# Edge attention in steps of one tile of 128 edges, softmax over 20 tiles at once, and a group's four placements interleaved with queries and relations

## The chip, the cores and the metric

The kernel runs on one core of one Trainium2 chip. The metric is the device time of one execution in microseconds (us). Before the change it is 1203.07 us, the median of three runs (1202.24 to 1210.01).

## The reference

One block of a graph network over 3125 nodes of 256 features, with three parts: attention over edges (4 heads of 64), a linear attention over all nodes, and a mixture of 8 experts of which each node takes two. The change lies in the edge attention. There are 53125 edges, sorted by their target node `dst`; a node's edges stand next to each other.

```
xn = layernorm(x)
Q, K, V = (xn + 0.1*query_emb) @ Wq + bq, ... Wk, ... Wv      # 3125 x 4 x 64
score[e,h] = sum_d Q[dst e] * (K[src e] + 0.2*rel_w[type e]) / 8
w          = softmax of score over the edges that share dst
agg[n]     = sum over edges e with dst e = n of w[e] * V[src e]
x = x + layernorm(agg @ Wo + bo + xn)*gamma + beta + linear_attention(xn)
x = x + experts(layernorm(x))
```

## The kernel before, in words

The program has five stages: projections and the step list (0 to about 170 us), edges (about 170 to 827 us), combination, routing, experts. The stages before and after the edges keep their work, apart from buffer addresses and the sizes of the step list.

**Tiles, steps and groups.** A tile is 128 edges, one per partition. Nodes are handled in 25 blocks of 128. A step holds edges of one block of nodes only, so the step list has one more entry for each change of block: with steps of 256 edges (two tiles) there are 208 + 24 = 232 steps, 464 tiles. The block of a step is known only at run time; its offsets are in one-partition rows in SBUF (`qRow`, `own_bank`, `next_bank`, `aRow`, `last_bank`), and an engine reads them into registers with `load_values` (line 92). A group is four tiles, two steps; there are 116. A chunk of the softmax is four groups, 16 tiles; there are 29.

**Scoring a group.** GpSimd gathers the key and value rows of each tile's sources (516 floats a row) into a ring `KV` of three chunks, 48 tiles, with an indirect DMA for each tile (line 668). Before a gather it waits until the placement of the tile that last had this place is done, and it is at most three groups ahead of the key addition. SyncE loads target and type rows. VectorE makes one-hots of them: `PT` (line 897), and for every second group `OT` (line 901). TensorE multiplies them with the node block's queries (`queries`, line 779, three bf16 parts, two tiles a call) and with the relations (`relations`, line 768). VectorE then adds the relations to the keys (`modify`, line 911), multiplies by the queries (`multiply`, line 918, twice) and sums by head (`reduce`, line 924).

**Softmax of a chunk.** It is a running maximum over edges of one target. TensorE turns the scores (`turn_scores`), VectorE scans them forward and backward (962, 968), the ends of the tiles go over a one-partition row (`turn_ends`, `ends`, `carry`, `carried`, `turn_carries`, `carry_in`), ScalarE takes exponentials (`exponents`), TensorE turns them back (`turn_weights`) and ScalarE copies them to `WS` (`weights`, which waits for its own copies at the end). This is spread over the four groups of the next chunk. When a chunk begins, VectorE rescales the sums so far (`rescale`, line 946).

**Summing.** Two chunks behind the scoring (8 groups), ScalarE multiplies the values by the weights, four activations a tile (`weigh`, line 684); in the last two chunks VectorE does it, two tiles at once (line 937). VectorE makes the placement matrices `PM` (`place`, line 929, two buffers), and TensorE adds the weighted values into one of three PSUM banks by the block of nodes (`aggregate`, line 811). Once a step, TensorE clears the bank that comes next (`clear`, line 798), and ScalarE copies the sums of the bank before to `ACC` (`copy_sums`, line 698); the copy waits for the placement of the step before (`s_pw`) and for its own copy before (`s_acc`).

**Order of the work.** It is written out by hand on each engine and tied by semaphores. In each group TensorE goes: register loads, queries of the first two tiles of the next group, clear and placement of a step, relations of the next group, queries of its last two tiles, clear and placement of the other step. VectorE goes: one-hots of the next group, `modify`, `place`, two `multiply` with small softmax instructions between, `reduce`. ScalarE: for each of two steps `weigh` and `copy_sums`, its register loads (`before`, line 687) once a group. When no group is left to score, the last two chunks are summed (`drain`). Then SyncE's load of the values of nodes (`VB`, line 652), issued when 216 steps are placed, has to be there for the next stage.

## Time and profile before

| | |
|---|---|
| median of the runs | 1203.07 us (1202.24 to 1210.01) |
| the profiled execution's own time | 1205.97 us |
| its span, first to last instruction | 1204.2 us |
| TensorE (PE) busy | 1019.1 us (85%) |
| VectorE (DVE) busy | 909.2 us (76%) |
| ScalarE (ACT) busy | 814.2 us (68%) |
| GpSimd (POOL) busy | 802.1 us (67%) |
| key additions of the edge stage | 116, starting at 184.8 to 795.5 us |

The profiled execution is one run under the hardware profiler; the sums are made against its times. Busy shares are means over stages with different limits. PEld is TensorE's weight load, which overlaps its multiplications; a name that ends in q is an engine's instruction sequencer, which runs ahead of the engine and also reads registers. "idle before <-" names what ended the idle time ahead of an instruction; "issue" is time in which the engine waited for nothing that the profile shows. Instructions of an engine overlap a little: the next starts before the last one is quite done.

### The profile page before, as it was taken

What the parts mean: (1) busy time and instruction counts of PE and PEld (TensorE: products, weight loads), DVE (VectorE), ACT (ScalarE), POOL (GpSimd) and SP (SyncE); (2) the same over time, 40 slices, a digit from 0 to 9 for tenths busy, and PEclk for the clock granted to TensorE, in tenths of its full rate; (3) what the DMA queues carried; (4) which work ended last, traced back from release to release, by engine and by line L of the source; (5) the groups of instructions that cost most, each with busy time, mean ns of one, the idle gap of its engine ahead of it and who ended that gap; (6) DMA issues with size and microseconds to landing.
All of it is one profiled execution on the core that took longest, in us unless ns stands there. A gap on an engine that the chain in (4) does not pass through costs nothing. (4 is left out here: it accounts for less than half of the span.)

```text
span 1204.2 us, 26894 instructions
## 1 busy us (share of the span) xinstructions
PE 1019.1 (85%) x6959; PEld 778.4 (65%) x6960; DVE 909.2 (76%) x1999; ACT 814.2 (68%) x2902; POOL 802.1 (67%) x873
## 2 busy tenths in 40 slices
PE   4899966888888888888888888878996489999993
PEld 3677744565565556555556565556895478999993
DVE  5777547999998999999999999985996823333331
ACT  3344410489888888898988889863675466766662
POOL 3667657777777777777777777712983347666662
PEclk9899975699998999999999999998997689999997
DMA  8333438888888888888888888876325724444445
GB/s 240 114 122 113 141 105 234 240 248 234 240 240 241 243 239 238 243 242 241 246 243 239 247 244 244 242 242 227 111 71 177 237 53 72 69 70 65 70 66 133
DMA packets 130432, 220.56 MB, mean 183 GB/s; under 512 B 24772, under 2 KB 89452, under 8 KB 129992
## 3 DMA queue, kind: packets, MB, share of 16 engines
q0 software_dynamic: 48832, 138.49, 42.9%
q1 hardware_dynamic: 81480, 80.63, 21.5%
q8 instruction: 55, 0.90, 0.3%
q14 instruction: 65, 0.53, 0.1%
HBM read 188.00 MB, written 34.25 MB: 185 GB/s over the span
## 5 line engine op out<-in xcount | busy, mean ns | idle before, releaser
L668 POOL DMA_INDIRECT KV<-kv,ixs x464 | 471.7, 1017 | 151.5 <-issue 110.9
L684 ACT ACTIVATE KV<-KV,WS 128x65 f32<-128x65 f32 x1728 | 437.2, 336 | 40.7 <-issue 40.6
L811 PE MATMUL ps_o<-KV,PM 128*128 128x260 f32 x928 | 255.5, 399 | 49.1 <-DVE PM L929 31.4
L785 PE MATMUL ps_qe<-Q,PT 128*128 x1392 | 209.6, 288 | 21.8 <-DVE PT L897 12.9
L811 PEld LDWEIGHTS ps_o<-KV,PM 128*128 128x128 f32 x928 | 160.4, 193 | 91.5 <-issue 73.0
L785 PEld LDWEIGHTS ps_qe<-Q,PT 128*128 128x128 bf16 x1392 | 122.4, 100 | 77.3 <-issue 46.5
L918 DVE TENSOR_TENSOR KV<-KV,ps_qe 128x512 f32<-128x512 f32 x232 | 149.5, 674 | 0.2
L911 DVE TENSOR_TENSOR KV<-KV,ps_u 128x1024 f32<-128x1024 f32 x116 | 140.0, 1207 | 12.8 <-DMA KV<-kv,ixs 12.5
L924 DVE TENSOR_REDUCE S<-KV 128x16 f32<-128x1024 f32 x116 | 138.7, 1196 | 1.1
L1705 DVE TENSOR_TENSOR YG<-ps_y,KV 128x256 f32<-128x256 f32 x56 | 23.8, 425 | 140.8 <-PE ps_y L1678 140.8
L1589 POOL DMA_INDIRECT acc<-YG,DX x56 | 88.7, 1583 | 61.3 <-issue 36.9
L1619 ACT ACTIVATE HT<-ps_h,WB 128x128 f32<-128x128 f32 x224 | 82.1, 367 | 58.4 <-PE ps_h L1662 45.9
L1662 PE MATMUL ps_h<-XT,WB 128*128 128x128 f32 x896 | 114.9, 282 | 0.0
L1662 PEld LDWEIGHTS ps_h<-XT,WB 128*128 128x128 f32 x896 | 105.8, 194 | 5.2 <-issue 2.4
L1678 PE MATMUL ps_y<-Q,HT 128*128 x448 | 105.8, 379 | 0.0
L698 ACT COPY ACC<-ps_o x231 | 81.6, 353 | 13.5 <-PE ps_o L811 11.2
L1678 PEld LDWEIGHTS ps_y<-Q,HT 128*128 128x128 f32 x448 | 80.9, 190 | 8.7
L775 PEld LDWEIGHTS ps_u<-rel,OT 64*128 64x128 bf16 x1392 | 49.5, 98 | 51.0 <-issue 46.9
L929 DVE TENSOR_TENSOR PM<-iota_f,DC 128x512 f32<-128x512 f32 x116 | 78.5, 677 | 1.7 <-PE ps_o L811 1.7
L1579 POOL DMA_INDIRECT XG<-xtab,GX x56 | 55.5, 992 | 25.5 <-issue 10.1
L775 PE MATMUL ps_u<-rel,OT 64*128 64x64 bf16 x1392 | 63.5, 195 | 10.1 <-DVE KV L911 6.5
L798 PE MATMUL ps_o<-nought 128*128 128x260 bf16 x230 | 63.5, 276 | 0.7 <-ACT ACC L698 0.5
(306 smaller groups left out, 1610.5 us busy)
## 6 DMA issues: line engine op xcount, KB each, us to landing
dlb<-dl_rows SPq DMA_DIRECT2D x116, 128.0 KB
tyb<-ty_rows SPq DMA_DIRECT2D x116, 64.0 KB
KV<-kv,ixs POOLq DMA_INDIRECT x464
kv<-kvb SPq DMA_DIRECT2D x25, 258.0 KB, 2.5
xs_rows<-xs SPq DMA_DIRECT2D x25, 256.0 KB, 2.5
KV<-xs_rows SPq DMA_DIRECT2D x10, 640.0 KB, 9.8
Q<-in_f_W_dram SPq DMA_DIRECT2D x8, 512.0 KB, 6.0
KV<-in_f_W_dram SPq DMA_DIRECT2D x8, 512.0 KB, 6.0
```

Source lines behind the costliest of these rows:

```text
L668: pool.indirect_dma_start(kv[:, c % KR, n, :], None, d["kv"], bass.IndirectOffsetOnAxis(ap=T["ixs"][:, c % KR, n:n + 1], axis=0)).then_inc ...
L684: m = a.activation(part, part, ACT.Copy, scale=W[:, c % 2, s * H + h:s * H + h + 1])
L775: m = pe.matmul(T["ps_u"][:, k * D:(k + 1) * D], T["OT"][half, G_ // 2 % 2, k * P:(k + 1) * P], T["rel3"][half, n, :], start=(n == 0), sto ...
L785: m = pe.matmul(T["ps_qe"][:, p % 3, k, :], T["PT"][:, h, (p % 2 * 2 + k) * P:(p % 2 * 2 + k + 1) * P], T["Q3"][:, bass.ds(at + n * C, C)] ...
L811: m = pe.matmul(ps_o[:, bass.ds(bank, A)], PM[:, p // 2 % 2, p % 2 * 2 + k, :], kv[:, c % KR, 2 * x + k, C:KVW], start=False, stop=True, s ...
L911: v.tensor_tensor(k, k, T["ps_u"][:, 0:G * D].rearrange("p (s d) -> p s d", s=G).unsqueeze(2).broadcast_to([P, G, H, D]), ALU.add).then_in ...
L918: v.tensor_tensor(k, k, T["ps_qe"][:, p % 3, :, :], ALU.mult).then_inc(s_mu, 1)
L924: v.tensor_reduce(S[:, c % 2, g * G * H:(g + 1) * G * H].rearrange("p (s h) -> p s h", h=H), keys(G_).rearrange("p s (h d) -> p s h d", h= ...
L1589: pool.indirect_dma_start(d["acc"], bass.IndirectOffsetOnAxis(ap=T["DX"][:, u, 0:1], axis=0), YG[:, u * C:(u + 1) * C], None, compute_op=A ...
L1619: a.activation(HT[:, u % 2, m, :], T["ps_h"][:, m, 0:SLOTS], ACT.Gelu, bias=WB[:, u % 2, 2 * HID + m:2 * HID + m + 1]).then_inc(s_hg, 1)
L1662: r = pe.matmul(T["ps_h"][:, m, 0:SLOTS], WB[:, u % 2, k * HID + m * P:k * HID + (m + 1) * P], XT[:, u % 2, k, :], start=(k == 0), stop=(k ...
L1678: r = pe.matmul(T["ps_y2"][:, (u % YB) * HB + w, 0:C], HT[:, u % 2, m, w * P:(w + 1) * P], T["W2"][:, bass.ds(at + m * C, C)], start=(m == ...
```

## The change

A step is now one tile of 128 edges. The step list has 416 + 24 = 440 steps and as many tiles, 110 groups of four. A softmax chunk is five groups, 20 tiles; there are 22. The ring keeps 48 tiles, no longer cut into chunks; the gathers take their indices from `SRC` itself, and ScalarE's index copies (line 677) go. Each tile has its own block: `queries` takes an offset for each tile, a bank is cleared and copied once a tile, and TensorE reads `qRow`, `own_bank` and `next_bank` four values at a time, once a group; ScalarE still reads two values at a time, now twice a group. Sums are 9 groups behind the scoring. TensorE's order in a group is: register loads, placement 0, queries, (turned scores), placement 1, relations, placement 2, (turned weights), queries, placement 3, each placement with its clear. VectorE weighs the fourth tile of every odd group, and in the last nine groups tiles 1 to 3. The separate drain is now part of the same loop. Counts in the preparation and the addresses of buffers that share memory with the ring follow; `VB` is loaded once 405 of 440 tiles are placed.

```diff
-TE = 2 * P
+TE = P
 ET = (E_REAL + TE - 1) // TE
 H, D = 4, 64
 NREL = 64
 MD = 32
 NS = ET + NT - 1
-SC = 2
+SC = 4
 SP_ = NS // SC
 G = 4
-CP = 8
-NCH = NS // CP
-CG = 2 * CP // G
-CB_ = 2 * CP
-KR = 3
+CB_ = 20
+NCH = NS // CB_
+CG = CB_ // G
+NG = NS // G
+RING = 48
+LAG = 9
 RO = 3
...
+    CAR, RRO, WO = P + 2 * B, P + 2 * B + 2, P + 2 * B + 8
+    NX = NG + LAG
+    def by_vector(g):
+        if g >= NG - LAG:
+            return ((1, 1), (2, 2))
+        return ((3, 1),) if g % 2 else ()
+    def by_scalar(g):
+        taken = [k + n for k, m in by_vector(g) for n in range(m)]
+        return [k for k in range(G) if k not in taken]
+    scalar_count, vector_count, a_n, v_n = {}, {}, 0, 0
+    for g in range(NG):
+        for k in by_scalar(g):
+            a_n += 1
+            scalar_count[g * G + k] = a_n
+        for k, m in by_vector(g):
+            v_n += 1
+            for n in range(m):
+                vector_count[g * G + k + n] = v_n
...
-            for c in range(NCH):
-                pool.wait_ge(s_ix, c + 1)
-                for g in range(CG):
-                    for k in range(G):
-                        n, scored = g * G + k, c * CG + g - AHEAD
-                        if k % 2 == 0:
-                            wait(pool, s_pw, (c - KR) * CP + 2 * g + k // 2 + 1)
-                        if k == 0:
-                            wait(pool, s_ku, scored + 1)
-                        if k == 2:
-                            wait(pool, s_sc, scored + 1)
-                        pool.indirect_dma_start(kv[:, c % KR, n, :], None, d["kv"],
-                                                bass.IndirectOffsetOnAxis(ap=T["ixs"][:, c % KR, n:n + 1], axis=0)).then_inc(s_g[(c * CG + g) % GS], 16)
+            for t in range(NS):
+                g = t // G
+                wait(pool, s_pw, t - RING + 1)
+                if t % G == 0:
+                    wait(pool, s_ku, g - AHEAD + 1)
+                pool.indirect_dma_start(kv[:, t % RING, :], None, d["kv"],
+                                        bass.IndirectOffsetOnAxis(ap=T["SRC"][:, t:t + 1], axis=0)).then_inc(s_g[g % GS], 16)
         @block.scalar
         def _(a):
-            def indices(c):
-                if c >= KR:
-                    last = (c - KR) * CG + CG - 1
-                    a.wait_ge(s_g[last % GS], 16 * G * (last // GS + 1))
-                a.copy(T["ixs"][:, c % KR, :], T["SRC"][:, c * CB_:(c + 1) * CB_]).then_inc(s_ix, 1)
-            def weigh(p):
-                c, x = divmod(p, CP)
-                for s in (2 * x, 2 * x + 1):
-                    for h in range(H):
-                        part = kv[:, c % KR, s, C + h * (D + 1):C + (h + 1) * (D + 1)]
-                        m = a.activation(part, part, ACT.Copy, scale=W[:, c % 2, s * H + h:s * H + h + 1])
+            def weigh(t):
+                for h in range(H):
+                    part = kv[:, t % RING, C + h * (D + 1):C + (h + 1) * (D + 1)]
+                    at = t % CB_ * H + h
+                    m = a.activation(part, part, ACT.Copy, scale=W[:, t // CB_ % 2, at:at + 1])
                 m.then_inc(s_wv, 1)
...
-                if q % CP == 0:
-                    a.wait_ge(s_rs, q // CP)
+                if q % CB_ == 0:
+                    a.wait_ge(s_rs, q // CB_)
...
+            for x in range(NX):
+                c, j = x // CG - 1, x % CG
+                g = x - LAG
+                softmax, summed = 0 <= c < NCH, g >= 0
+                for k in range(G):
+                    t = g * G + k
+                    if summed:
+                        if k % 2 == 0:
+                            at, bank = before(max(t - 1, 0))
+                        if k in by_scalar(g):
+                            weigh(t)
+                        if t >= 2:
+                            copy_sums(t - 1, at[k % 2], bank[k % 2])
+                    if softmax and j == 1 and k == 1:
+                        ends(c)
+                if softmax and j == 2:
+                    exponents(c)
+                if softmax and j == 3:
+                    weights(c)
+            at, bank = before(NS - 2)
+            copy_sums(NS - 1, at[1], bank[1])
+            a.wait_ge(s_pw, NS)
+            a.wait_ge(s_acc, NS - 1)
...
+                return load_values(nc, mybir.EngineType.PE, T["qRow"][0:1, G * G_:G * G_ + G], (NT - 1) * 3 * C)
+            def banks(name, t, n):
+                return load_values(nc, mybir.EngineType.PE, T[name][0:1, t:t + n], 2 * 512)
...
+            def aggregate(t, bank):
+                g = t // G
+                pe.wait_ge(s_pm, g + 1)
+                if t in vector_count:
+                    pe.wait_ge(s_wd, vector_count[t])
                 else:
-                    pe.wait_ge(s_wv, p + 1)
-                if x == 0:
-                    wait(pe, s_rs, c)
-                for k in range(2):
-                    m = pe.matmul(ps_o[:, bass.ds(bank, A)], PM[:, p // 2 % 2, p % 2 * 2 + k, :], kv[:, c % KR, 2 * x + k, C:KVW],
-                                  start=False, stop=True, skip_group_check=True)
-                m.then_inc(s_pw, 1)
+                    pe.wait_ge(s_wv, scalar_count[t])
+                if t % CB_ == 0:
+                    wait(pe, s_rs, t // CB_)
+                pe.matmul(ps_o[:, bass.ds(bank, A)], PM[:, g % 2, t % G, :], kv[:, t % RING, C:KVW],
+                          start=False, stop=True, skip_group_check=True).then_inc(s_pw, 1)
...
+            for x in range(NX):
+                c, j = x // CG - 1, x % CG
+                g, G_ = x - LAG, x + 1
+                softmax, summed, scored = 0 <= c < NCH, g >= 0, G_ < NG
+                if scored:
+                    at = rows(G_)
+                if summed:
+                    own = banks("own_bank", g * G, G)
+                    after = banks("next_bank", max(g * G - 1, 0), G)
+                    shift = 1 if g == 0 else 0
+                def add(k):
+                    t = g * G + k
+                    if summed:
+                        if t >= 2:
+                            clear(t - 1, after[k - shift])
+                        aggregate(t, own[k])
+                if softmax and j == 1:
+                    turn_ends(c)
+                if softmax and j == 2:
+                    turn_carries(c)
+                add(0)
+                if scored:
+                    queries(2 * G_, at[0:2])
+                if softmax and j == 0:
+                    turn_scores(c)
+                add(1)
+                if scored:
+                    relations(G_)
+                add(2)
+                if softmax and j == 3:
+                    turn_weights(c)
+                if scored:
+                    queries(2 * G_ + 1, at[2:4])
+                add(3)
         @block.vector
         def _(v):
@@ -901,8 +878,8 @@
...
+            def place(g):
+                wait(v, s_pw, (g - 1) * G)
+                v.tensor_tensor(PM[:, g % 2, :, :], T["iota_f"][:, :].unsqueeze(1).broadcast_to([P, G, P]),
+                                T["DC"][:, G * g:G * g + G].unsqueeze(2).broadcast_to([P, G, P]), ALU.is_equal).then_inc(s_pm, 1)
+            def weigh(g, k, n):
+                t = g * G + k
+                c, at = t // CB_, t % CB_ * H
                 v.wait_ge(s_w, 2 * c + 2)
-                part = kv[:, c % KR, 2 * x:2 * x + 2, C:KVW].rearrange("p s (h d) -> p s h d", h=H)
-                w = W[:, c % 2, 2 * x * H:(2 * x + 2) * H].rearrange("p (s h) -> p s h", h=H)
-                v.tensor_tensor(part, part, w.unsqueeze(3).broadcast_to([P, 2, H, D + 1]), ALU.mult).then_inc(s_wd, 1)
+                s0 = t % RING
+                part = kv[:, s0:s0 + n, C:KVW].rearrange("p s (h d) -> p s h d", h=H)
+                w = W[:, c % 2, at:at + n * H].rearrange("p (s h) -> p s h", h=H)
+                v.tensor_tensor(part, part, w.unsqueeze(3).broadcast_to([P, n, H, D + 1]), ALU.mult).then_inc(s_wd, 1)
             def rescale(c):
...
+            for x in range(NX):
+                c, j = x // CG - 1, x % CG
+                g = x - LAG
+                softmax, summed, scored = 0 <= c < NCH, g >= 0, x < NG
+                if x + 1 < NG:
+                    onehots(x + 1)
+                if scored:
+                    modify(x)
+                if g > 0 and g % CG == 0:
+                    rescale(g // CG)
+                if summed:
+                    place(g)
+                if softmax and j == 2:
+                    carry_in(c, 0)
+                if scored:
+                    multiply(2 * x)
+                elif summed:
+                    weigh(g, *by_vector(g)[0])
+                if softmax and j == 2:
+                    carry_in(c, 1)
+                if scored:
+                    multiply(2 * x + 1)
+                if softmax and j == 0:
+                    run_forward(c)
+                if softmax and j == 1:
+                    carry(c)
+                if softmax and j == 2:
+                    differences(c)
+                if summed:
+                    for k, n in by_vector(g)[0 if scored else 1:]:
+                        weigh(g, k, n)
+                if scored:
+                    reduce(x)
+                if softmax and j == 0:
+                    run_backward(c)
+                if softmax and j == 1:
+                    carried(c)
...
```

## Rows read from the trace of the kernel before

**Rows 1.** Windows of the core: busy time of each engine, clock, DMA share.

```profile
400.00:500.00 100.00, 85.81 (x694) 60.14 (x691) 98.66 (x178) 89.67 (x373) 76.06 (x76) 1.00 0.84 242
```

**Rows 2.** Groups of instructions, VectorE, 300 to 700 us: busy, mean ns | idle before.

```profile
L918 DVE TENSOR_TENSOR KV<-KV,ps_qe 128x512 f32<-128x512 f32 x151 | 97.4, 674 | 0.0
L924 DVE TENSOR_REDUCE S<-KV 128x16 f32<-128x1024 f32 x76 | 90.8, 1195 | 0.7
L911 DVE TENSOR_TENSOR KV<-KV,ps_u 128x1024 f32<-128x1024 f32 x75 | 90.4, 1206 | 2.3 <-DMA KV<-kv,ixs 2.0 <-PE ps_u L775 0.3
L929 DVE TENSOR_TENSOR PM<-iota_f,DC 128x512 f32<-128x512 f32 x75 | 50.8, 677 | 0.0
L897 DVE TENSOR_SCALAR PT<-dlb,iota_p 128x512 bf16<-128x512 bf16 x75 | 31.1, 414 | 0.0
L901 DVE TENSOR_SCALAR OT<-tyb,iota_t 128x512 bf16<-128x512 bf16 x37 | 12.3, 334 | 0.0
```

**Rows 3.** Single lines: ns min/median/max, first and last start (first row 460 to 790).

```profile
L962 DVE TENSOR_TENSOR_SCAN SF<-BR,ps_s x16: 401/403/405, 467.7 to 783.3; 64x128 f32<-64x128 bf16 x16
...
L911 DVE TENSOR_TENSOR KV<-KV,ps_u x116: 1194/1206/1222, 184.8 to 795.5; 128x1024 f32<-128x1024 f32 x116
...
L929 DVE TENSOR_TENSOR PM<-iota_f,DC x116: 656/677/693, 229.5 to 823.1; 128x512 f32<-128x512 f32 x116
```

**Rows 4.** Timeline of VectorE: start us, us, instruction.

```profile
459.69 1.21 DVE L911 TENSOR_TENSOR KV<-KV,ps_u 128x1024 f32<-128x1024 f32 x1
460.82 0.68 DVE L929 TENSOR_TENSOR PM<-iota_f,DC 128x512 f32<-128x512 f32 x1
```

**Rows 5.** Single line 937, VectorE's weighting of two tiles.

```profile
L937 DVE TENSOR_TENSOR KV<-KV,WS x16: 662/692/695, 802.2 to 824.3; 128x520 f32<-128x520 f32 x16
```

**Rows 6.** Waits, 300 to 700 us: total, times, longest.

```profile
PE ps_o L811 <- DVE PM L929: 22.8, 36, 1.4
```

**Rows 7.** Timeline of ScalarE.

```profile
459.15 2.03 ACT L684 ACTIVATE KV<-KV,WS 128x65 f32<-128x65 f32 x8 [0.46 <-issue]
...
461.35 2.02 ACT L684 ACTIVATE KV<-KV,WS 128x65 f32<-128x65 f32 x8
...
465.03 2.03 ACT L684 ACTIVATE KV<-KV,WS 128x65 f32<-128x65 f32 x8 [1.09 <-issue]
```

**Rows 8.** Groups of instructions, GpSimd's gathers, 400 to 500 us.

```profile
L668 POOL DMA_INDIRECT KV<-kv,ixs x76 | 76.7, 1009 | 24.2 <-issue 17.7 <-DVE KV L911 3.7 <-PE ps_o L811 1.4
```

**Rows 9.** Line 92, register loads: `qRow`, `aRow` two values each, `off` one.

```profile
L92 PEldq TENSOR_LOAD <-qRow x116: 529/545/733, 174.7 to 789.6; - x116
...
L92 ACTq TENSOR_LOAD <-aRow x116: 480/491/682, 226.9 to 825.1; - x116
...
L92 ACTq TENSOR_LOAD <-off x56: 273/279/407, 963.4 to 1178.9; - x56
L92 PEldq TENSOR_LOAD <-off x56: 297/302/465, 968.6 to 1181.2; - x56
```

**Rows 10.** Line 1556, SyncE's register loads in the experts, four values each.

```profile
L1556 SPq TENSOR_LOAD <-turn_i x13: 295/298/513, 991.8 to 1171.4; - x13
```

**Rows 11.** Timeline of ScalarE in the drain.

```profile
807.35 0.38 ACT L698 COPY ACC<-ps_o  x1 [0.18 <-ACT ACC L698]
808.55 0.38 ACT L698 COPY ACC<-ps_o  x1 [0.83 <-ACT ACC L698]
...
827.01 0.38 ACT L764 COPY ACC<-ps_o 128x260 f32<-128x260 f32 x1 [0.30 <-PE ps_o L811]
```

**Rows 12.** Timeline of TensorE around a group's end.

```profile
458.50 1.04 PE L811 MATMUL ps_o<-KV,PM 128*128 128x260 f32 x4
459.83 0.87 PE L785 MATMUL ps_qe<-Q,PT 128*128 x6 [0.28 <-DVE PT L897]
```

**Rows 13.** Line 92, 457 to 461 us: the start of this group's first load.

```profile
L92 PEldq TENSOR_LOAD <-qRow x1: 547/547/547, 457.8 to 457.8; - x1
```

More of the change, by code:

```diff
@@ L758, in _ @@
-            drain(NCH)
-            drain(NCH + 1)
-            at, bank = before(NP - 2)
-            copy_sums(NP - 1, at[1], bank[1])
-            a.wait_ge(s_pw, NP)
-            a.wait_ge(s_acc, NP - 1)
+            for x in range(NX):
[17 more added lines that the diff above has]
+                    weights(c)
@@ L888, in _ @@
-            drain(NCH)
-            drain(NCH + 1)
+            queries(0, at[0:2])
+            queries(1, at[2:4])
+            for x in range(NX):
[32 more added lines that the diff above has]
+                add(3)
```

282 lines of the change are left out of this document (66 added, 216 removed).

## The prediction, on record before the result was known

> **What bounds the kernel now.** I first read the busy time of each engine over a stretch in the middle of the edge stage: VectorE is busy 98.66 us of 100, ScalarE 89.67, TensorE 85.81, and TensorE has its full clock [rows 1]. VectorE's own rows show that it waits for almost nothing [rows 2]. So the stage goes at VectorE's rate. The scoring addition (line 911) starts 116 times from 184.8 to 795.5 us: 610.7 us for 115 intervals, 5.31 us for a group of four tiles [rows 3]. The stage is half of the span, so the change is priced by how many groups there are, by what a group costs on VectorE, by whether TensorE or ScalarE then takes longer, and by the ramp and the drain.
>
> A group on VectorE: 1.206 + 2 x 0.674 + 1.195 + 0.677 + 0.414 and half of 0.334 for the type one-hots, which come every second group, is 5.01 us [rows 2]. Each instruction starts 0.08 us before the one ahead of it ends (459.69 to 460.82 is 1.13 us for a duration of 1.21) [rows 4], six and a half times: 4.48 us. A chunk of the softmax takes (783.3 - 467.7) / 15 = 21.04 us [rows 3]; less four groups, 3.1 us are left for its small instructions and waits.
>
> **The change, part by part.**
> *Fewer tiles.* A step was two tiles; 208 + 24 steps are 464 tiles in 116 groups. Now 416 + 24 steps are 440 tiles in 110 groups. The queries, relations, gathers and row loads go down by the same 5%.
> *Softmax over 20 tiles.* 22 chunks take the place of 29. The instructions work on 80 partitions instead of 64 with as many columns (the carry scans have 88 for 72); I add 0.1 us a chunk: 3.2 us for five groups, 0.64 a group where it was 0.78.
> *Weighting of one tile in every second group moves to VectorE.* A two-tile weighting is 0.692 us [rows 5]; one tile half of it, about 0.33 from start to start, 2.5 times a chunk: 0.83 us. It lies on the bound itself.
> *The order on TensorE.* The first placement of a group now stands ahead of the queries and needs PM, which VectorE finishes some 2.1 us into its group (one-hots 0.33, addition 1.13, PM 0.6). TensorE already waits for PM, 22.8 us in 400 [rows 6], but had its queries ahead of that wait. Behind it now stand queries, turned scores, relations. The relations end about 2.3 us later (placement and clear 0.55 twice, queries 0.7, relations 0.45), 4.4 us into the group, and the next addition wants them at 5.7: hidden; a TensorE more than 1 us late would uncover it. The turned scores land at 2.1 + 0.55 + 0.7 + 0.3 = 3.7 us, and VectorE's forward scan asks for them at 3.3: 0.4 us of new wait a chunk. A chunk: 5 x 4.48 + 3.2 + 0.83 + 0.4 = 26.8 us, 5.37 a group. I take 5.39, with something for the turned carries, which also arrive later.
> *Twice the bank clears and copies of sums.* TensorE: two more clears a group; a four-tile placement's distance shows a clear at 0.11 to 0.27 us, so +0.2 to +0.5 on 4.5 us of busy time a group (85.81 over 19): at most 5.0, under 5.39. ScalarE: eight activations and a copy go from 459.15 to 461.35, 2.20 us [rows 7]; with 0.25 for the copy, a tile is 0.97. A group was 4.4 us and is 3.5 x 0.97 + 4 x 0.25 = 4.4, plus some 3.3 us a chunk for the softmax's copies, exponentials and their waits (1.09 us of them is the reload behind the weights, [rows 7]): 5.06 us. Both hidden by VectorE, ScalarE with 0.3 us to spare.
> *Gathers.* 76 of them have 76.7 us busy and 17.7 us of issue [rows 8], 1.25 us each, 5.0 a group: under 5.39 still. They now wait for a placement at every tile instead of every second, 12 groups behind; the data is wanted three groups later. Zero, and if the cover went, POOL's 5.0 would still be below. The index copy on ScalarE goes (0.1 us a chunk, hidden). SP's queue loads fewer rows and only four break rows for five groups: zero, it waits for VectorE.
> *Register loads.* This is the term that the trace leaves open. TensorE's sequencer reads block offsets and two bank rows for each group, two values each, at 0.545 us; one value costs it 0.302. ScalarE: 0.491 for two, 0.279 for one [rows 9]. So a second value costs 0.21 to 0.24 us. Now each of TensorE's three loads has four values. By that increment one is 0.302 + 3 x 0.24 = 1.02 us; but SP loads four values in 0.298 us [rows 10]. Bounds 0.30 and 1.02. The only row with four values is the nearest one, and I take it for the two aligned loads; the bank load that starts one value off may be the slow one. Then a group has 0.3 + 0.3 + (0.3 to 1.02), no more than the 1.63 of before. ScalarE keeps two values a load and makes four loads for two: 1.96 us of sequencer time a group, read ahead while activations run (there is no gap between the two blocks of eight [rows 7]). Zero, unless its placement waits hold the sequencer back.
> The Trainium skill, DMA: Bandwidth & Descriptors (Latency and other measured facts), says of such loads that there is a floor and that unrolling four times amortizes it; SP's row agrees in kind, its floor of 600 ns is above every row here.
> *Ramp.* Placements started 229.5 us in, the ninth addition 1.2 before it at 228.3 [rows 3]: eight intervals of 5.44. Now there are nine before sums begin: 49 us. Then 100 x 5.39 = 539. Together 588, against 610.7: -22.7.
> *Preparation.* The counting pass has twice the columns and four rounds, and the single-partition rows 440 columns instead of 232: a few us of VectorE, nearly all while it waits for TensorE's first projections; +1.
> *Drain.* Before, from the last addition at 795.5 to the last copy at 827.0: 31.5 us [rows 3, 11]. There ScalarE's copies come in pairs: 808.55 - 807.35 = 1.20 us where two register loads lie between, 0.56 within a pair. Then it was TensorE that set the rate. Now a pair is two tiles, not four. A group is 2 x (1.20 + 0.56) plus the one tile it still weighs, 0.97: 4.5 us on ScalarE, more than the other engines have. Nine groups of 4.5, 5.4 to finish the last scored group and 1.2 for the end: 47.1. +15.6.
> Sum: -22.7 + 1 + 15.6 = -6. All other stages stay. Against the profiled execution's 1205.97 (span 1204.2) that gives about 1200, and against the median of the runs, 1203.07, **1197 us**.
>
> **The rivals.**
> *Forecast, within a per cent or so (0.43)*: as above; with waits at their bounds (nothing or 0.9 us a chunk, the drain 4 or 5 us a group) 1185 to 1212.
> *TensorE becomes the bound through its register loads (0.26).* Each four-value load costs 1.02 us, three with their gaps 3.2. For it: two engines, same increment. Against: SP's four. The sequencer starts them when it has passed the last placement's waits: at 457.8, with TensorE's last placements of that group running 458.50 to 459.54 and the next queries at 459.83 [rows 12, 13]. So it runs some 1.7 us ahead of the array. With 4.3 us of array work, 3.5 of loads and address arithmetic, and 1.3 to 2 us of them covered, a group takes 5.8 to 6.5 us. It decides from the point where a load exceeds about 0.85 us. 100 groups x (0.4 to 1.1) = +40 to +110: 1237 to 1307, around 1270, slower. The Trainium skill, Runtime: NRT & Kernel Launch (Instruction fetch mechanics), gives about 200 ns a register even in bulk; the two-value rows agree, SP's does not; by that rule this rival would come true.
> *ScalarE sets the rate (0.14).* With 5.06 of 5.39 used, its copy must see the placement of one tile before, where it used to see that of a two-tile step before; if half of a load pair (0.98) is uncovered each group it becomes 5.55 to 5.7. 100 x 0.15 to 0.3: 1212 to 1230. For it: its 1.09 us gap; against: loads run ahead elsewhere.
> *More is won than I count (0.17).* No wait for the turned scores, a drain at the 3.6 us of the load pairs alone: -10 and -8: about 1181.
>
> **The numbers.** About 1% (12 us) is what a measurement of this kernel can tell from no change. Faster by more: 0.17, and 0.10 of the forecast's own lower part: 0.27. Within: 0.33 of the forecast and 0.04 of the ScalarE case: 0.37. Slower: TensorE 0.26, ScalarE 0.10: 0.36. The range reaches from 1183 to 1275: some 0.06 below, and above it nearly half of the TensorE case, 0.12.
>
> **What would show it.** 110 additions with 5.39 us between starts, VectorE at 98% or more in the middle; four-value loads at 0.3 us; a short VectorE wait for TensorE's turned scores; 45 to 49 us from the last addition to the last copy. Loads near 1 us, VectorE waiting for relations or queries, and TensorE's loads just before each first placement would make it wrong; so would ScalarE without idle time.

## The result and the profile after

The changed kernel takes **1249.22 us** (median of 4 runs, 1247.76 to 1249.33) against 1202.65 us for the kernel before in the same job: a ratio of **1.038 (1.032 to 1.044)**, slower. The forecast was 1197 us.

The spans of the two profiled executions are 1204.2 and 1247.4 us, so 43.2 us are to be found. The first view of the kernel after is single lines: nanoseconds min/median/max, then first and last start. The scoring addition, line 911 before, is line 888 here.

```profile
L888 DVE TENSOR_TENSOR KV<-KV,ps_u x110: 1194/1206/1222, 189.3 to 820.7; 128x1024 f32<-128x1024 f32 x110
L95 PEldq TENSOR_LOAD <-qRow x110: 327/332/526, 179.3 to 816.0; - x110
L95 PEldq TENSOR_LOAD <-own_bank x110: 325/329/343, 235.6 to 863.3; - x110
L95 PEldq TENSOR_LOAD <-next_bank x110: 328/1004/1037, 236.0 to 863.7; - x110
L95 ACTq TENSOR_LOAD <-aRow x220: 479/487/686, 235.8 to 867.5; - x110
```

The addition runs 110 times in 631.4 us where [rows 3] has 116 in 610.7: 5.79 us for a group, against 5.31 before and a forecast of 5.39. By stretches:

| us | before | forecast | after |
|---|---|---|---|
| first addition starts | 184.8 | 185.8 | 189.3 |
| first to last addition | 610.7 | 588 | 631.4 |
| last addition to last copy | 31.5 | 47.1 | 48.4 |
| last copy to the end of the span | 377.2 | the same | 378.3 |

Nearly the whole miss is the middle row: 43.4 us above the forecast. The drain is 1.3 above it and the preparation 3.5.

The same stretch of the edge stage as in [rows 1], of the kernel after (busy us of TensorE, its weight loads, VectorE, ScalarE, GpSimd; clock; DMA share; GB/s):

```profile
400.00:500.00 100.00, 81.91 (x644) 55.46 (x644) 90.42 (x161) 83.58 (x327) 71.74 (x70) 1.00 0.77 220
```

No engine is full any more. VectorE went from 98.66 to 90.42, TensorE from 85.81 to 81.91, at full clock. So the group is not longer because some engine has more to do: engines wait for one another. The waits of the kernel after from 300 to 700 us (total, times, longest) say where:

```profile
POOL KV L685 <- PE ps_o L801: 79.8, 157, 1.8
...
DVE SF L942 <- PE ps_s L807: 23.5, 13, 2.3
...
PE ps_o L801 <- DVE PM L906: 14.9, 26, 0.8
DVE ps_o L926 <- PE ps_o L801: 13.7, 13, 1.2
```

VectorE waits mostly in two places, once in each chunk of the softmax: 23.5 us for the turned scores ahead of the forward scan (`SF`), and 13.7 us for a placement ahead of the rescaling of the sums. GpSimd's gathers wait much longer for placements than before (79.8 us), but no wait of VectorE for a gather shows in this kernel. VectorE's groups of instructions over the same 400 us (busy us, mean ns, idle before) confirm that the rest of its work is as counted, and that the relations (`ps_u`) are never late:

```profile
L888 DVE TENSOR_TENSOR KV<-KV,ps_u 128x1024 f32<-128x1024 f32 x69 | 83.2, 1206 | 0.3 <-PE ps_u L765 0.3
...
L917 DVE TENSOR_TENSOR KV<-KV,WS 128x260 f32<-128x260 f32 x34 | 14.0, 412 | 0.0
...
L942 DVE TENSOR_TENSOR_SCAN SF<-BR,ps_s 80x128 f32<-80x128 bf16 x14 | 5.8, 416 | 25.6 <-PE ps_s L807 23.5 <-issue 2.1
```

25.6 us over 14 chunks is 1.83 us a chunk at the scan, where the forecast had 0.4; 13.7 over 14 is 0.98 at the rescaling, where it had nothing. Together 2.8 us, 2.4 more than forecast. The chunk has grown from the forecast's 26.8 to about 29 us (5 x 5.79), 2.2 more: the waits account for it.

What makes the turned scores late is in the timeline of the kernel after around one scan (start, us, instruction, idle before):

```profile
475.96 0.70 PE L801 MATMUL ps_o<-KV,PM 128*128 128x260 f32 x2
...
476.50 0.82 PE L776 MATMUL ps_qe<-Q,PT 128*128 x6
...
477.31 0.70 PE L801 MATMUL ps_o<-KV,PM 128*128 128x260 f32 x2
...
479.28 0.28 PE L789 MATMUL ps_o<-nought 128*128 128x260 bf16 x1 [1.27 <-ACT ACC L708]
...
479.57 0.70 PE L801 MATMUL ps_o<-KV,PM 128*128 128x260 f32 x2
...
480.11 0.82 PE L776 MATMUL ps_qe<-Q,PT 128*128 x6
...
480.76 0.27 PE L807 MATMUL ps_s<-ident,S 128*80 128x128 f32 x1
...
481.14 0.42 DVE L942 TENSOR_TENSOR_SCAN SF<-BR,ps_s 80x128 f32<-80x128 bf16 x1 [2.26 <-PE ps_s L807]
```

And the register loads of that group, line 95 of the kernel after, 474 to 480 us:

```profile
L95 PEldq TENSOR_LOAD <-qRow x1: 334/334/334, 477.3 to 477.3; - x1
L95 PEldq TENSOR_LOAD <-own_bank x1: 328/328/328, 477.7 to 477.7; - x1
L95 PEldq TENSOR_LOAD <-next_bank x1: 1017/1017/1017, 478.1 to 478.1; - x1
```

Read them together. The group's last placement starts at 477.31, and the first load at 477.3: as I read it, TensorE's sequencer begins the loads when it has passed the waits of the last placement. They end at 479.1, and the next group's first clear runs at 479.28. The loads' cover, that is the work which TensorE's array (the part that multiplies) still has in hand while they run, is here one placement of 0.7 us, against 1.8 us of loads; 1.27 us are idle. Before, the loads began at 457.8 with four instructions of placement for two tiles still to run, and the array resumed with queries after 0.28 us [rows 12, 13]. The profile puts those 1.27 us down to a copy of ScalarE (`ACT ACC`); ScalarE's last copy ahead of the clear ended at 478.54, and the loads' rows are what fills the gap.

This group is among the worst. TensorE's idle time at this place, ahead of whatever comes first behind the loads, can be added up from its waits of 300 to 700 us. In the kernel before these are the turned ends (822), the turned carries (827) and the first queries (785):

```profile
PE ps_s L822 <- issue: 11.4, 17, 0.7
...
PE ps_qe L785 <- DVE PT L897: 6.4, 19, 0.4
PE ps_qe L785 <- issue: 4.9, 18, 0.4
PE ps_s L827 <- issue: 4.4, 17, 0.3
```

In the kernel after they are the same two turns (811, 816) and the first clear (789):

```profile
PE ps_o L789 <- ACT ACC L708: 28.9, 27, 1.3
...
PE ps_s L816 <- issue: 13.3, 14, 1.3
PE ps_s L811 <- issue: 10.0, 14, 0.8
PE ps_o L789 <- issue: 4.9, 13, 0.6
```

That is 27.1 us in 75 groups before, 0.36 us a group, and 57.1 us in 69 groups after, 0.83 us a group. The three loads together last as long as they did, 1.67 us for 1.62: what has shrunk is their cover.

### The profile page after: what moved, and what is told of

It reads as the page before. It is cut to its first block and busy times, and to the rows that moved or that the text cites. A ratio compares the mean times of both kernels' runs of the same rounds, so it can differ in the third digit from the quotient of the medians.

```text
span 1247.4 us, 28148 instructions
## 1 busy us (share of the span) xinstructions
PE 1026.5 (82%) x6923; PEld 771.9 (62%) x6924; DVE 887.7 (71%) x1938; ACT 812.8 (65%) x2770; POOL 790.6 (63%) x851
## 5 line engine op out<-in xcount | busy, mean ns | idle before, releaser
L685 POOL DMA_INDIRECT KV<-kv,SRC x440 | 457.4, 1040 | 183.6 <-PE ps_o L801 109.2
L694 ACT ACTIVATE KV<-KV,WS 128x65 f32<-128x65 f32 x1452 | 387.2, 339 | 71.2 <-issue 69.0
L801 PE MATMUL ps_o<-KV,PM 128*128 128x260 f32 x880 | 287.7, 410 | 31.7 <-DVE PM L906 24.5
L776 PE MATMUL ps_qe<-Q,PT 128*128 x1320 | 193.8, 287 | 5.3 <-DVE PT L874 5.0
L801 PEld LDWEIGHTS ps_o<-KV,PM 128*128 128x128 f32 x880 | 134.2, 192 | 68.3 <-issue 51.4
L708 ACT COPY ACC<-ps_o x439 | 156.6, 357 | 29.2 <-PE ps_o L801 22.5
L789 PE MATMUL ps_o<-nought 128*128 128x260 bf16 x438 | 122.6, 280 | 53.9 <-ACT ACC L708 42.2
L776 PEld LDWEIGHTS ps_qe<-Q,PT 128*128 128x128 bf16 x1320 | 131.3, 101 | 52.5 <-issue 10.9
L895 DVE TENSOR_TENSOR KV<-KV,ps_qe 128x512 f32<-128x512 f32 x220 | 141.8, 676 | 0.3
L789 PEld LDWEIGHTS ps_o<-nought 128*128 128x128 bf16 x438 | 42.4, 97 | 91.4 <-issue 82.2
L765 PEld LDWEIGHTS ps_u<-rel,OT 64*128 64x128 bf16 x1320 | 47.1, 98 | 50.0 <-issue 45.6
```

The source lines that it names most:

```text
L685: pool.indirect_dma_start(kv[:, t % RING, :], None, d["kv"], bass.IndirectOffsetOnAxis(ap=T["SRC"][:, t:t + 1], axis=0)).then_inc(s_g[g % ...
L694: m = a.activation(part, part, ACT.Copy, scale=W[:, t // CB_ % 2, at:at + 1])
L708: a.copy(ACC[:, bass.ds(at, A)], ps_o[:, bass.ds(bank, A)]).then_inc(s_acc, 1)
L776: m = pe.matmul(T["ps_qe"][:, p % 3, k, :], T["PT"][:, h, (p % 2 * 2 + k) * P:(p % 2 * 2 + k + 1) * P], T["Q3"][:, bass.ds(at[k] + n * C, ...
L789: pe.matmul(ps_o[:, bass.ds(bank, A)], T["nought"][:, 0:P], T["nought"][:, 0:A], start=True, stop=True, skip_group_check=True).then_inc(s_ ...
L801: pe.matmul(ps_o[:, bass.ds(bank, A)], PM[:, g % 2, t % G, :], kv[:, t % RING, C:KVW], start=False, stop=True, skip_group_check=True).then ...
```

## The experiments

Theory A: the loads' cover is gone, and their duration reaches VectorE once a chunk, through the turned scores. Theory B: TensorE's delay is paid in each group. A third: take one wait away and another takes its place. After the first four runs theory A was widened to A': loads on TensorE and on ScalarE, and the place of the first placement, each cost by themselves, and their costs add. Ratios are against the kernel before in the same job, whose median was 1200.03 us for the first four runs, 1202.34 for the next four and 1204.08 for the last four. Gains in us are differences of medians; across jobs they hold to about 3 us (by the ratios, the 20, 19 and 17 us of experiments 1, 4 and 3 are 19, 17 and 16).

**1. The slow load made fast.** `next_bank` is stored one value further on, so that its four values start on a multiple of four.

```
-                    after = banks("next_bank", max(g * G - 1, 0), G)
-                    shift = 1 if g == 0 else 0
+                    after = banks("next_bank", g * G, G)
+                    shift = 0
...
-                   "next_bank": ((1, NS), I32)
+                   "next_bank": ((1, NS + 4), I32)
```

> The changed kernel with one thing different: the row next_bank is stored one value further on, so that TensorE's four-value load of it starts at a multiple of four values like the other two. In the changed kernel it took 1.00 us and the two others 0.33. Expected: 0.33 us for all three. Theory A (a chain once a chunk: ScalarE's late weights in the fifth group, then TensorE's register loads that cannot start before its fourth placement has its weights, then placement 0, queries, turned scores, VectorE's forward scan): 0.67 us less a chunk on that chain, 22 x 0.67 = 15 us, so 1249 becomes 1230 to 1236. Theory B (TensorE's loads bound every group): 0.67 us in each of some 100 groups until VectorE is full again, so about 1249 - 57 = 1192 to 1200. Theory C (ScalarE's throughput bounds): no change, 1246 to 1250.

Measured: **1229.1 us, 1.023 (1.019 to 1.027)**, 20 us less than the kernel after. The same line in this kernel's trace:

```profile
L95 PEldq TENSOR_LOAD <-next_bank x110: 326/328/350, 236.7 to 845.3; - x110
```

The load fell from 1.004 to 0.328 us by where its first value lies and nothing else. That is 74 us of sequencer time in all and 20 us of the kernel: 0.18 us a group, 0.9 a chunk. Theory B wanted nearly all of it, some 50 us of the kernel; as a sum for every group it is out. TensorE's idle time at the loads fell from 57.1 to 18.5 us (300 to 700 us), while its waits for PM ahead of placements rose from 14.9 to 36.5: a good part of what the shorter load frees is spent in the next wait. VectorE's scan still waits 16.8 us in 14 chunks, so the long load was not the only cause.

**2. The turned scores taken out from behind the loads.** They are issued at the start of their group, ahead of its loads and its first placement.

```
+                if softmax and j == 0:
+                    turn_scores(c)
                 if scored:
                     at = rows(G_)
...
-                if softmax and j == 0:
-                    turn_scores(c)
                 add(1)
```

> The changed kernel, with TensorE turning the scores at the very start of the group, before its register loads and its first placement, instead of behind placement 0 and the first queries. VectorE's forward scan waited 36.7 us for them over 20 chunks. Theory A (the wait is paid once a chunk because of where the turned scores stand in TensorE's order): that wait goes to below 0.1 us a chunk, some of it comes back as a wait for the relations or queries; 22 x 1.2 to 1.7 = 26 to 37 us, so 1212 to 1223. Theory B (TensorE's loads bound every group): the wait moves to another instruction of VectorE and the time stays within 5 us of 1249. Theory C (ScalarE's throughput bounds): likewise 1245 to 1250.

Measured: **1246.9 us, 1.037 (1.034 to 1.041)**, only 2 us less. The waits of this kernel, 300 to 700 us:

```profile
DVE SM L971 <- PE ps_s L817: 11.5, 14, 1.2
...
DVE KV L888 <- PE ps_u L765: 8.6, 15, 0.9
...
DVE EC L953 <- ACT EZ L713: 5.2, 14, 0.4
```

The wait at the scan is gone from the answer, and its 23.5 us came back as 11.5 at the turned carries (`SM`, 1.9 in the kernel after), 8.6 at the relations and 5.2 at ScalarE's copy of the turned ends (`EZ`). So "once a chunk, through the turned scores" was too narrow, and my first theory fell with it; theory B had said that the time would stay. What VectorE pays is that TensorE as a whole is late; the scan is only the first place in the chunk that shows it.

**3. The order of before.** The queries, turned scores and, between second and third placement, relations stand as the kernel before has them; all else is the kernel after.

```
-                add(0)
                 if scored:
                     queries(2 * G_, at[0:2])
                 if softmax and j == 0:
                     turn_scores(c)
+                add(0)
                 add(1)
                 if scored:
                     relations(G_)
-                add(2)
                 if softmax and j == 3:
                     turn_weights(c)
                 if scored:
                     queries(2 * G_ + 1, at[2:4])
+                add(2)
                 add(3)
```

> The changed kernel, with TensorE's order within a group as it was before the change: queries, turned scores, placements 0 and 1, relations, turned weights, queries, placements 2 and 3. Steps of one tile, loads and softmax chunks as in the changed kernel. Theory A (position of placement 0 ahead of queries and turned scores costs once a chunk): the forward scan's wait falls by the placement's 0.8 us and PM's wait no longer stands ahead of the queries; 15 to 25 us less, 1224 to 1234. Theory B (loads bound every group): the loads have two placements ahead of them instead of one and can be covered by 0.5 us more: up to 30 us less. Theory C (ScalarE): no change. A rival to all, that the interleaving itself is worth something: slower than 1249.

Measured: **1232.52 us, 1.025 (1.021 to 1.029)**, 17 us less, of which 15 lie between first and last addition (616.2). In this kernel's waits the scan has 8.4 us in 7 chunks where it had 23.5 in 13:

```profile
DVE SF L942 <- PE ps_s L807: 8.4, 7, 1.5
```

**4. ScalarE's loads.** Two loads of four values a group, both starting on a multiple of four, in place of four loads of two.

```
-                        if k % 2 == 0:
-                            at, bank = before(max(t - 1, 0))
+                if summed:
+                    at, bank = before(g * G, G)
...
-                            copy_sums(t - 1, at[k % 2], bank[k % 2])
+                            copy_sums(t - 1, at[k], bank[k])
```

> The changed kernel, with ScalarE reading its two rows four values at a time, aligned, once a group: 2 loads of about 0.31 us for 4 of 0.49 us (1.96 us of its sequencer's time a group becomes 0.62). Theory A: the reload behind the weights' copies is on the chain once a chunk, 0.98 becomes 0.62: 22 x 0.36 = 8 us, and the drain's groups, which I priced at 2 x (1.20 + 0.56) + 0.97 = 4.5 us, become 3.3 to 3.6: 8 to 10 us; together 1230 to 1236. Theory B (TensorE's loads bound every group): only the drain's part, 1239 to 1243. Theory C (ScalarE's throughput bounds every group through its loads): its activations wait for issue 42 us in 400 now; with these gone 1200 to 1215.

Measured: **1230.66 us, 1.024 (1.021 to 1.028)**, 19 us less: 10.6 in the loop (620.8) and 6.5 in the drain (852.04 - 810.1 = 41.9). ScalarE's loads in this kernel:

```profile
L95 ACTq TENSOR_LOAD <-aRow x111: 292/308/517, 235.1 to 850.8; - x111
L95 ACTq TENSOR_LOAD <-last_bank x111: 277/305/313, 235.6 to 851.1; - x111
```

1.95 us of loads a group became 0.61. The forecast had put their cost in the loop at zero.

**5. TensorE's loads moved ahead of the last queries.** The long load stays. If the place of the loads is all that matters, three more pieces of array work stand behind them.

```
                 if softmax and j == 3:
                     turn_weights(c)
+                if x + 1 < NX:
+                    ahead = registers(x + 1)
                 if scored:
                     queries(2 * G_ + 1, at[2:4])
                 add(3)
```

> The changed kernel, with TensorE's three register loads (their lengths as they are: 0.33, 0.33 and 1.00 us) issued one placement earlier: for the next group, ahead of the second queries, not behind the fourth placement. Theory A' (not the length but the place of the loads costs: the sequencer cannot begin them until the fourth placement has its weights, and nothing is queued behind that placement to cover them): they are covered by queries and the fourth placement, so at least the 20 us that the shorter load gave, 1215 to 1228. Theory B' (the sequencer's total time is what counts): 1245 to 1250. Theory C' (ScalarE's chain sets the time, TensorE's loads only fill its wait): 1240 to 1249.

Measured: **1336.94 us, 1.114 (1.109 to 1.119)**, 88 us more than the kernel after, where 20 to 35 less was expected. A clean miss. TensorE's timeline in this kernel:

```profile
454.94 0.28 PE L789 MATMUL ps_o<-nought 128*128 128x260 bf16 x1
455.24 0.70 PE L801 MATMUL ps_o<-KV,PM 128*128 128x260 f32 x2
457.37 0.91 PE L776 MATMUL ps_qe<-Q,PT 128*128 x6 [1.43 <-issue]
```

and its loads there:

```profile
L95 PEldq TENSOR_LOAD <-qRow x1: 333/333/333, 455.3 to 455.3; - x1
...
L95 PEldq TENSOR_LOAD <-next_bank x1: 1009/1009/1009, 456.1 to 456.1; - x1
```

The third placement (455.24) has waits of its own. As I read the times, the sequencer is held there until the operands are in, so it starts the loads at 455.3 with one placement ahead of the array, as at the group's end, and the queries behind them can't be handed over until 457.1. This kernel's waits of 300 to 700 us, some 60 groups, have 60 such waits, 71.3 us in all or 1.2 a group, where the kernel after has 0.83 at its loads:

```profile
PE ps_qe L776 <- issue: 48.3, 43, 1.5
...
PE ps_qe L776 <- DVE PT L880: 23.0, 17, 1.5
```

The idle array also lost clock:

```profile
400.00:500.00 100.00, 78.44 (x551) 51.18 (x551) 78.41 (x137) 73.60 (x284) 62.09 (x60) 0.93 0.69 190
```

The mean granted clock is 0.93 here, at 78.44 us busy, where the kernel after holds 1.00; between full speed and half of it (2.4 and 1.2 GHz) that is a seventh of the stretch at the lower. Part of the 88 us is that; how much was not separated.

**6. Both loads short** (1 and 4 together).

> The changed kernel with both shorter loads: TensorE's third one aligned (1.00 becomes 0.33 us) and ScalarE's four-value loads (4 x 0.49 becomes 2 x 0.33 a group). Alone they gave 20 and 18 us, 8 or so of the latter in the drain. Theory A' (the two lie one behind the other on one chain that closes once a chunk, over ScalarE's weights and TensorE's placements): the gains add, 1210 to 1214. Theory C' (each engine has a limit of its own and the larger one counts): 1218 to 1226.

Measured: **1212.5 us, 1.008 (1.005 to 1.010)**, 37 us less than after; 20 and 19 by themselves. The gains add, as A' has it. Loop 605.8, last addition to last copy 40.7.

**7. Both loads short and both moved forward**: TensorE's as in 5, ScalarE's behind the copy of the second tile.

```
+                    if summed and k == 1 and g + 1 < NG:
+                        ahead = before((g + 1) * G, G)
```

> As e6_loads_short, and both engines' loads issued ahead of the work that could cover them: TensorE's for the next group ahead of the second queries, ScalarE's behind the copy of the second tile. Theory A' (register loads, by length and place, are what the changed kernel has lost against its forecast of 1197): 1192 to 1203. Theory C' (the order of TensorE's work and the single-tile placements cost without the loads as well): it stays above 1208. If it lands under 1190, twenty tiles a softmax and 440 tiles are worth more than I counted.

Measured: **1218.75 us, 1.012 (1.009 to 1.016)**, 6 us more than without the moves, where 9 to 20 less was expected. Short loads make the wrong place cheap, not right. Which of the two moves costs was not separated.

**8. The same with the order of before** (7 and 3).

> As e7_loads_all, with TensorE's order of before: queries, turned scores, placements 0 and 1, relations, turned weights, queries, placements 2 and 3. With the loads as they were, this order gave 17 us. Theory A' (that gain was cover for the loads): with the loads hidden it makes no difference, within 4 us of e7. Theory D (placement 0 ahead of the queries costs by itself, since it waits for PM and holds up the turned scores and relations): 8 to 20 us less than e7. Rival: the interleaved order is the better one once the loads are out of the way: slower than e7 by more than 4 us.

Measured: **1196.36 us, 0.995 (0.994 to 0.997)**; loop 590.8. The order is worth 22 us on top of short loads.

**9. Short loads in their own place, and the order of before** (6 and 3).

> The changed kernel with the short loads of e6 and TensorE's order of before (queries ahead of placement 0), loads where the changed kernel has them, at the group's start. e6 is 1212, e10 (same order, loads issued earlier) 1196. If the order gives its 17 to 22 us by itself (theory D), this is 1190 to 1196, and not above e10, since issuing the loads earlier only empties TensorE (as e5 showed, 88 us slower). If the earlier loads were what helped in e10: 1203 or more.

Measured: **1193.9 us, 0.992 (0.990 to 0.994)**. It is 0.8% below the kernel before; its interval is clear of 1, as that of experiment 8 is, though the gain is less than the 1% that the prediction calls telling. Its scoring additions:

```profile
L891 DVE TENSOR_TENSOR KV<-KV,ps_u x110: 1195/1207/1223, 188.1 to 776.1; 128x1024 f32<-128x1024 f32 x110
```

588.0 us for 109 intervals, 5.39 each. The stretch of [rows 1] in this kernel:

```profile
400.00:500.00 100.00, 89.60 (x692) 59.85 (x691) 96.93 (x171) 89.71 (x355) 77.37 (x75) 1.00 0.82 236
```

and VectorE's waits, 300 to 700 us:

```profile
DVE KV L891 <- DMA KV<-kv,SRC: 9.1, 14, 1.2
...
DVE ps_o L929 <- PE ps_o L804: 2.2, 5, 0.6
```

The wait for the turned scores is gone and that at the rescaling fell from 13.7 to 2.2 us. What is left is one wait a chunk for a gather, 0.6 us each.

**10. The kernel before with a long load.** Its last load of a group reads four values that start one off, in place of two; two of the values are not used.

```
-                        after = banks("next_bank", p - 1)
+                        after = load_values(nc, mybir.EngineType.PE, T["next_bank"][0:1, p - 1:p + 3], 2 * 512)
```

> The kernel before the change with one thing different: TensorE's load of next_bank reads four values at an odd place, about 1.00 us instead of 0.53, the two values more are not used. Theory A' (in the order of before, a load has two placements ahead of it and VectorE as the bound, so 0.5 us more a group is covered): at most 4 us slower, ratio under 1.004. Theory B' (what TensorE's sequencer needs is paid in every group): 0.47 x 108 = 50 us slower, ratio 1.04.

Measured: **1207.23 us, 1.0025 (1.0002 to 1.0048)**, 3 us more than 1204.08. The trace shows the load at full length:

```profile
L92 PEldq TENSOR_LOAD <-next_bank x115: 531/1007/1036, 232.0 to 830.0; - x115
```

It is 0.47 us longer in the 107 groups that the edit reaches (the other eight loads, in the drain, still read two values). That is 50 us of sequencer time, and 3 us are paid, where in the kernel after 74 us cost 20. But not because the load is covered here. TensorE's waits in this kernel, 300 to 700 us:

```profile
PE ps_qe L786 <- issue: 25.2, 36, 1.0
PE ps_s L823 <- issue: 18.1, 17, 1.2
PE ps_s L828 <- issue: 12.3, 19, 0.8
PE ps_o L812 <- DVE PM L930: 7.7, 14, 1.3
PE ps_qe L786 <- DVE PT L898: 3.1, 4, 0.8
```

The idle time at the loads is 58.7 us where the kernel before has 27.1: 0.42 us for each of 75 groups, nearly all of the added length. In return the wait for PM ahead of the placements fell from 22.8 us [rows 6] to 7.7. TensorE comes later to a wait that it had anyway, and VectorE, which sets the rate, hardly pays. So the kernel before had slack behind its loads. The kernel after has less cover (0.83 us idle for 0.36) and also less of that slack (14.9 us of waits for PM). How its 20 us divide between the two was not measured.

**11. The drain.** Experiment 9, and VectorE weighs four of four tiles in the last nine groups, where it weighed three.

```
         if g >= NG - LAG:
-            return ((1, 1), (2, 2))
+            return ((0, 2), (2, 2))
```

> As e11, and in the last nine groups VectorE weighs all four tiles, ScalarE none. The drain took 48.6 us from the last addition to the last copy in the changed kernel, at 4.3 us a group on ScalarE (two load pairs, one tile weighed, four copies). With four-value loads and no tile to weigh a group is 4 x 0.56 + 0.4 = 2.6 to 2.9 us: 5 to 9 us less than e11, 1183 to 1189. If copies wait for TensorE's placements instead, 2 us less at most.

Measured: **1190.48 us, 0.990 (0.988 to 0.992)**: 3 us less than 9, last addition to last copy 35.6 us for 38.7. Expected were 5 to 9 less, so something else holds a part of the drain; what it is was not followed. It is the best version found.

**12. Moves and drain** (8 and 11).

> e10 with the drain of e13, to set the two places of the loads side by side in the order with queries first. If the earlier loads cost (as in e5 and e7) even here, it is 3 to 10 us slower than e13; if they are harmless with two placements behind them, within 3 us of it.

Measured: **1194.1 us, 0.992 (0.990 to 0.994)**, 4 us above 11 in the same job: moving the loads forward doesn't pay in any version. Experiment 7's verdict holds with the better order too.

## Why the prediction was wrong, point by point

**The failed step is "Register loads", and its conclusion of zero.** The durations were taken rightly: 0.3 us for the two aligned loads, up to 1.02 for the one that starts one value off, measured 0.332, 0.329 and 1.004. Their sum, 1.67 us a group, is nearly what it was before (1.62). From an unchanged sum I concluded an unchanged cost, and left out what stands between the last instruction that waits and the loads: two tiles of placement before, one now. My own rival had written down that mechanism and its 1.7 us of lead [rows 12, 13], and priced it only for three loads of 1.02 us ("It decides from the point where a load exceeds about 0.85 us"). It decided with one long load. What the runs show in place of zero: idle time at the loads of 0.83 us a group where it was 0.36, and 20 us of the kernel for the length of the one long load (experiment 1). In the order of before a load made longer in the same way cost 3 us, since a wait for PM took the delay up (experiment 10); with the loads moved to right behind another waiting instruction the kernel took 88 us more (experiment 5).

**ScalarE's doubled loads were not zero either.** "Read ahead while activations run" holds only while nothing ahead of them waits. Each copy of sums now waits for the placement of one tile before, and the loads follow it; so I read it, the run itself shows only what their length costs. Measured: 19 us, 10.6 of them between first and last addition and 6.5 in the drain, whose forecast had counted the loads (experiment 4). The rival of 1212 to 1230 (1227, by its own sum) named this condition; its price of 15 to 30 us was for the loop, and of that 10.6 came. What it called ScalarE setting the rate was not: ScalarE is busy 83.58 of 100.

**"The order on TensorE ... hidden" was wrong by 15 to 22 us.** I followed the queries and the relations to the instruction that wants them and found slack for each by itself, with the loads ahead of them taken as free. Relations are indeed never late. But the turned scores come 1.83 us late a chunk, not 0.4. Ahead of them stand the loads, and then the first placement with waits for PM and for ScalarE's weighting of its own; experiments 1, 3 and 4 each made that wait shorter (16.8, 8.4 and 17.3 us for 23.5). The order alone returned 17 us (experiment 3), and 22 and 19 with short loads.

The three terms add up: 20, 19 and 17 us by themselves are 56; together they take the kernel from a ratio of 1.038 to 0.992, 55 us (experiment 9). Within the loop they are 19.6, 10.6 and 15.2 us, 45.4 for the 43.4 by which it missed the forecast.

**What was right.** Fewer groups and longer chunks are worth what was counted: in experiment 9, without the three terms, the loop is 588.0 us, the forecast's figure, at 5.39 us a group; VectorE's weighting, clears, copies and gathers are all within it. In that version TensorE is busy 0.896 x 5.39 = 4.8 us a group and ScalarE the same, under the 5.0 and 5.06 allowed. That 588 falls together to the last digit is partly luck: VectorE is busy 96.9, not 98, it waits for gathers, which I had at zero, and that kernel is not the one that was forecast: TensorE has the order of before and shorter loads. The drain's mechanism and size were right, 48.4 for 47.1, with a group at 4.33 us for 4.5.

**The preparation** took 4.5 us more, not 1. Single lines of the kernel after show why in part: the single-partition rows, 440 columns for 232, cost more than twice as much each, and they follow one another on VectorE.

```profile
L310 DVE TENSOR_SCALAR qRow<-ps_gram x1: 937/937/937, 25.1 to 25.1; 1x440 int32<-1x440 f32 x1
L311 DVE TENSOR_SCALAR aRow<-ps_gram x1: 921/921/921, 26.1 to 26.1; 1x440 int32<-1x440 f32 x1
```

Before they took 0.38 and 0.39 us. The 4.5 us was not followed further, and from run to run the first addition moved by 3 us (187.2 to 190.4) in versions with nearly the same preparation.

**The range and the chances.** 1249 lies in the range, and there by the TensorE rival, whose price of 1237 to 1307 had the wrong make-up: I gave it every group at 0.4 us or more, from loads that were all slow, and it came from one slow load, ScalarE's loads and the order together. Left open: a version with the new order in which the first placement's operands are ready earlier was not tried, so the order's cost is shown by taking it back, not by curing it; the share of the clock in experiment 5; and what ScalarE's loads hold up.

## What to carry to other kernels

In these traces a register load on TensorE's own queue was covered only by work handed over before and with the last instruction that waited: look in the trace at when the sequencer starts it, and at the idle time behind it, not at its sum per iteration. What is left uncovered costs time only as far as no later wait takes it up: look for that wait too. When an order is split into smaller steps, count again the work that is in hand when the loads begin. Shortening the loads (four values at once, first value on a multiple of four) paid here, and moving them to a place behind another waiting instruction made it worse. A wait that shows at one line, once a chunk, may be the engine behind it being late all the time: taking that line out of the queue only moves the wait.

## What the runs showed of the hardware that was not expected

In these traces a register load's time goes by the number of values and by where the first one lies, counted from the start of its row. On TensorE's queue one value takes 0.302 us, two take 0.545 [rows 9], four that start on a multiple of four 0.33, and four that start three past a multiple of four 1.004 (the same in experiment 10, where they start one or three past, 1.007); SP's row of four at 0.298 [rows 10] is of the fast kind, and ScalarE's four took 0.31 where two took 0.487. So four values can be cheaper than two. One shift of the array brought the long load's median from 1.004 to 0.328 and its longest to 0.350 (experiment 1). The kernel after holds the same comparison by itself: its very first load of `next_bank` starts at value 0 and took 0.328. Two values are not fast on a multiple of four: the loads of `qRow` before start at even places, every second one at a multiple of four, and the shortest took 0.529 [rows 9]. Four values that start two past a multiple of four no run here shows.

The Trainium skill, Runtime: NRT & Kernel Launch (Instruction fetch mechanics), gives about 200 ns a register even for loads in bulk; it writes of the runtime's own loads from HBM, and the rows here lie in SBUF. The two-value rows and the shifted four-value load agree with it (0.23 us for each further value); the aligned ones, at 0.08 us a value, do not, and by that rule experiments 1 and 4 would have gained nothing.
